# Normalised causal convolution over 16 channels: VectorE's third of the streamed units given to ScalarE and GpSimd

## The chip, the cores and the metric

The kernel runs on one core of one Trainium2 chip. The metric is the device time of one execution in microseconds; of three executions of the kernel before the median is 2928.14 us.

## What is computed

The input `x` has 16 channels of 2048 x 2048 in fp32. Channels form 8 groups of 2. The reference, cut to what matters:

```python
# layer 0
xm = where(tril, gn(x), 0)                      # gn: mean and variance over a group of 2 channels
y  = depthwise_conv(xm, weight, 6 x 11 taps)    # one filter per channel
x1 = x + where(tril, y, 0)
# layer 1
bias[h, i, j] = table(i - j)[h]                 # a small MLP of the position difference
out = x1 + gn(x1) + bias
```

The second normalisation is a scale and an offset per group, so `out = x1 * s + (bias + o)`. Above the diagonal the convolution is zero and `x1` is `x`.

## The kernel before

**Stages.** The program runs over stages, one per group and a few more. In a stage three groups are in work: the statistics of group s (`do_a`), normalisation and convolution of group s-1 (`do_b`), and the output of group s-2 (`do_c`). Stages 2 to 6 are one loop body, executed five times; stages 0, 1, 7, 8 and 9 are written out. Stages 0 and 1 produce no output, 8 has no statistics, and 9, the tail, only finishes output of the last group. A steady stage is called a lap below.

**Positions.** A stage has 90 positions n, one for each convolution tile of a group (2 channels, 4 bands of 512 rows, strips of columns). Each engine's program is written position by position, and each engine works it off in order. At position n ScalarE casts the transposed tile n+2 (L560), normalises tile n+4 (L545), squares finished pieces (L582), and then handles the output of group s-2. VectorE makes the low halves of tile n+2 (L696), masks and adds the convolution of tile n-1 (L709, L711), and then finishes output and takes statistics of `abuf` (L724). GpSimd masks tile n+4 where the diagonal runs through it (`mask_tile`, L940), copies the halo columns (L963, L955) and then adds bias (L971). TensorE transposes (L1022) and convolves (L1036) tile by tile, three tiles in flight.

**Output units.** Parts of `x1` that are kept in SBUF are finished in place by VectorE (`finish_kept`, L863, "kept blocks"), stored, and their place reloaded for the next group. All else is streamed: 36 units of 512 KB per group go through a ring of four buffers `ubuf` (`NUB`). SP loads a unit (L473) once the unit four before it in the ring has been stored. Then there are two ways to finish it:

- on ScalarE and GpSimd: `scale_stream` (L602, ScalarE, times s) and `add_bias` (L971, GpSimd, plus bias), stored from ScalarE's queue two positions later;
- on VectorE: `finish_stream` (L871), one instruction that does both, stored one position later.

The store itself is `store_stream` (L609) on ScalarE's queue, with a wait for the unit's finish. At one position ScalarE's program has the scalings first and the stores behind them. All queues are strictly in order, SP's too.

**What sets the order.** The table of constants before `plan` gives positions. `plan` spreads the loads, the uses and the stores of the units over the positions with a budget of bytes per position; a unit's position is `p.u[u]`, its load two positions before it or as soon as the store of unit u-4 is past. `U_ON_DVE(n, u)` says which way a unit takes. It is evaluated once for a steady lap and the same choice holds in every stage. These lines depend on it:

```python
p.u_load.append(max(at - 2, p.u_store[u - NUB] + 1) if u >= NUB else 0)
p.on_dve.append(on_dve[u] if on_dve else U_ON_DVE(p.u[u], u))
p.u_store.append(min(p.u[u] + (1 if p.on_dve[u] else 2), NT - 1))
```

In a group 13 units are VectorE's: 3, 7, 11, 15, 17, 19, 23, 27, 29, 31, 33, 34, 35. The last two are at position 87. The reload of the bias table (`load_bias`, L507, SP) waits for all additions and finishes of a channel.

Of the kernel before, what the change touches and what calls it, by code (L numbers as in the profile page):

```python
# [25 lines left out]
def preact_conv_kernel(nc, x, wflip, w1, b1, w2, b2, w3, b3, out):  # L26
# [84 lines left out]

    U_WEIGHT = lambda n: 1.8 if n < 10 else 1.5 if n > 82 else 1.0

    U_ON_DVE = lambda n, u: n > 85 or (u % 2 == 1 if n > 78 or 36 < n < 42 else u % 4 == 3)
    NEXT_BIAS_LOAD = 89


# [46 lines left out]
    def plan(do_a, do_b, do_c, on_dve=None):  # L164
# [40 lines left out]
        if do_c:  # L205
            for c, (lo, hi) in enumerate(U_WINDOW):
                for at in spread(NU // 2, 1.0, lo, hi, U_WEIGHT if do_a else lambda n: 1.0):
                    u = len(p.u)
                    p.u_load.append(max(at - 2, p.u_store[u - NUB] + 1) if u >= NUB else 0)
                    p.u.append(min(max(at, p.u_load[u] + 1, p.u[-1] if u else 0), hi))  # L210
                    p.on_dve.append(on_dve[u] if on_dve else U_ON_DVE(p.u[u], u))
                    p.u_store.append(min(p.u[u] + (1 if p.on_dve[u] else 2), NT - 1))
# [906 lines left out]
```

## Time and profile before

| | |
|---|---|
| median of 3 executions | 2928.14 us (2927.49 to 2932.59) |
| the profiled execution | 2927.91 us |
| its span | 2926.2 us |
| VectorE busy | 2305.1 us (79%) |
| TensorE matmul busy | 2044.5 us (70%) |
| ScalarE busy | 1674.6 us (57%) |
| GpSimd busy | 1158.7 us (40%) |
| DMA traffic | 916.61 MB, 313 GB/s in the mean |
| L602 and L971, each | 184 instructions |
| L871 | 104 instructions |

An engine's busy share says how much of the span it had an instruction in work. A row of the trace gives the start, the duration and, in brackets, how long the engine had been idle before and what released it. The rows used stand in a section below.

### The profile page before, as it was taken

What the parts mean: (1) busy time and instruction counts of PE and PEld (TensorE: products, weight loads), DVE (VectorE), ACT (ScalarE), POOL (GpSimd) and SP (SyncE); (2) the same over time, 40 slices, a digit from 0 to 9 for tenths busy, and PEclk for the clock granted to TensorE, in tenths of its full rate; (3) what the DMA queues carried; (4) which work ended last, traced back from release to release, by engine and by line L of the source; (5) the groups of instructions that cost most, each with busy time, mean ns of one, the idle gap of its engine ahead of it and who ended that gap; (6) DMA issues with size and microseconds to landing.
All of it is one profiled execution on the core that took longest, in us unless ns stands there. A gap on an engine that the chain in (4) does not pass through costs nothing.

```text
span 2926.2 us, 81475 instructions
## 1 busy us (share of the span) xinstructions
PE 2044.5 (70%) x28880; PEld 1944.5 (66%) x28880; DVE 2305.1 (79%) x4167; ACT 1674.6 (57%) x3051; POOL 1158.7 (40%) x1988
## 2 busy tenths in 40 slices
PE   4098887876677776777768876787767778888600
PEld 0098877776677776777657776776767777787500
DVE  6788888788778888789788887878987886767624
ACT  2066665656466665666456565575656666676621
POOL 1033234534335343543345344353434534454433
PEclk9999998999788898999889897899989998899855
DMA  8885749998699987989789997999889895878798
GB/s 260 293 303 164 285 149 382 364 328 329 241 367 350 367 323 293 376 326 358 277 334 363 326 345 252 367 363 358 311 315 370 332 349 197 311 255 295 280 342 331
DMA packets 316269, 916.61 MB, mean 313 GB/s; under 512 B 39280, under 2 KB 39280, under 8 KB 313936
## 3 DMA queue, kind: packets, MB, share of 16 engines
q1 hardware_dynamic: 201952, 595.03, 56.9%
q10 hardware_dynamic: 114048, 318.80, 28.7%
q8 instruction: 71, 1.16, 0.2%
q14 instruction: 198, 1.62, 0.2%
HBM read 594.18 MB, written 319.68 MB: 312 GB/s over the span
## 4 chain that ended last, share of the span: by engine, by line
DMA 38%; DVE 26%; issue 15%; PE 8%; ACT 6%; POOL 2%; SPq 2%; ACTq 1%; DVEq 0%; POOLq 0%
DMA ubuf<-in_x 11%; DMA out<-kept_c_band 9%; DVE entries L724 9%; DMA out<-ubuf 7%; PE psY L1036 6%; DVE kept_c_band L863 4%; DVE XT L696 4%; DMA ubuf<-out 4%; DMA abuf<-in_x 3%; DVE psY L709 3%; DMA kept_c_band<-in_x 3%; DVE kept_c_band L711 2%; ACT junk L582 2%; PE psT L1022 2%; ACT XT L560 2%
## 5 line engine op out<-in xcount | busy, mean ns | idle before, releaser
L1036 PEld LDWEIGHTS psY<-wsplit,XT 128*128 128x128 f16 x25920 | 1658.2, 103 | 291.7 <-DVE band L711 87.1
L1036 PE MATMUL psY<-wsplit,XT 128*128 128x168 f16 (+5 forms) x25920 | 1680.7, 226 | 233.7 <-DVE kept_c_band L711 98.8
L696 DVE TENSOR_TENSOR XT<-psT,XT 128x512 f16<-128x512 f32 x720 | 491.8, 683 | 372.4 <-ACT XT L560 370.5
L1022 PE MATMUL psT<-ident,xn 128*128 128x128 f32 x2880 | 500.9, 301 | 355.3 <-POOL xn L940 261.1
L560 ACT CAST XT<-psT 128x512 f16<-128x512 f32 x720 | 414.1, 575 | 455.6 <-PE psT L1022 260.1
L971 POOL TENSOR_TENSOR ubuf<-ubuf,bias 128x1024 f32<-128x1024 f32 x184 | 415.4, 2258 | 573.4 <-ACT ubuf L602 572.5
L724 DVE BATCH_NORM_STATS2 entries<-abuf 128x6 f32<-128x512 f32 x928 | 589.5, 682 | 62.4 <-DMA abuf<-in_x 61.3
L940 POOL TENSOR_TENSOR xn<-xn,mask 128x512 f32<-128x512 f32 x336 | 422.8, 1258 | 517.7 <-ACT xn L545 439.5
L1022 PEld LDWEIGHTS psT<-ident,xn 128*128 128x128 f32 x2880 | 331.6, 151 | 369.4 <-POOL xn L940 263.5
L545 ACT ACTIVATE xn<-kept_c_band,normp 128x512 f32<-128x512 f32 (+2 forms) x496 | 398.5, 803 | 109.3 <-DMA kept_c_band<-in_x 75.8
L963 POOL COPY halo<-XT 128x16 f16<-128x16 f16 x720 | 209.8, 291 | 634.1 <-DVE XT L696 619.3
L602 ACT ACTIVATE ubuf<-ubuf,outp 128x1024 f32<-128x1024 f32 x184 | 210.1, 1143 | 338.0 <-DMA ubuf<-in_x 228.5
L863 DVE SCALAR_TENSOR_TENSOR kept_c_band<-kept_c_band,outp,bias 128x1024 f32<-128x1024 f32 x224 | 348.6, 1569 | 38.8 <-ACT bias L652 38.8
L582 ACT ACTIVATE junk<-kept_c_band,cur 128x512 f32<-128x512 f32 (+2 forms) x464 | 311.9, 672 | 78.4 <-DVE kept_c_band L711 42.2
L711 DVE SCALAR_TENSOR_TENSOR kept_c_band<-psY,wback,kept_c_band 128x472 f32<-128x472 f32 (+3 forms) x496 | 344.6, 695 | 6.2
L871 DVE SCALAR_TENSOR_TENSOR ubuf<-ubuf,outp,bias 128x1024 f32<-128x1024 f32 x104 | 153.8, 1484 | 114.5 <-DMA ubuf<-in_x 64.2
L709 DVE TENSOR_TENSOR psY<-psY,mask 128x472 f32<-128x472 f32 (+2 forms) x336 | 204.1, 607 | 0.0
L545 ACT ACTIVATE xn<-band,normp 128x512 f32<-128x512 f32 (+1 forms) x224 | 174.3, 779 | 34.9 <-DVE normp L790 34.9
L955 POOL COPY XT<-halo 128x16 f16<-128x16 f16 x720 | 167.2, 232 | 27.3 <-PE psY L1036 23.2
L582 ACT ACTIVATE junk<-band,cur 128x512 f32<-128x512 f32 x192 | 131.9, 687 | 44.4 <-DVE cur L795 21.3
L711 DVE SCALAR_TENSOR_TENSOR band<-psY,wback,band 128x472 f32<-128x472 f32 (+2 forms) x224 | 150.5, 672 | 5.7
L582 ACT ACTIVATION_READ_ACCUMULATOR junk<-kept_c_band,cur 128x1 f32 x464 | 87.1, 188 | 0.0
(76 smaller groups left out, 445.0 us busy)
## 6 DMA issues: line engine op xcount, KB each, us to landing
abuf<-in_x SPq DMA_DIRECT2D x464, 512.0 KB, 7.3
out<-ubuf ACTq DMA_DIRECT2D x288, 512.0 KB, 6.4
kept_c_band<-in_x SPq DMA_DIRECT2D x112, 1024.0 KB, 7.8
out<-kept_c_band ACTq DMA_DIRECT2D x112, 1024.0 KB, 7.8
ubuf<-in_x SPq DMA_DIRECT2D x192, 512.0 KB, 6.3
band<-in_x SPq DMA_DIRECT2D x48, 1024.0 KB, 9.7
out<-band ACTq DMA_DIRECT2D x48, 1024.0 KB, 7.9
ubuf<-out SPq DMA_DIRECT2D x96, 512.0 KB, 6.6
```

Source lines behind the costliest of these rows:

```text
L545: last = nc.scalar.activation(to[:, :, 0:whole, :], slot(c, b)[:, :, x0:x0 + XC * whole].rearrange("p k (i c) -> p k i c", c=XC), ACT.Iden ...
L560: nc.scalar.copy(XT[:, n % NB3, 0, :, 2:P + 2], psT[n % NB3][:, :, :]).then_inc(hi_ready, 1)
L582: nc.scalar.activation(junk[:, 0:nr * (c1 - c0)].rearrange("p (r c) -> p r c", r=nr), slot(c, b)[:, r:r + nr, BW * q + c0:BW * q + c1], AC ...
L696: nc.vector.tensor_tensor(XT[:, n % NB3, 1, :, 2:P + 2], psT[n % NB3][:, :, :], XT[:, n % NB3, 0, :, 2:P + 2], ALU.subtract).then_inc(lo_r ...
L709: nc.vector.tensor_tensor(y, y, mask_at(b, t, c0, c1), ALU.mult).then_inc(conv_masked, 1)
L711: nc.vector.scalar_tensor_tensor(out=xs, in0=y, scalar=col(wback, c), in1=xs, op0=ALU.mult, op1=ALU.add, accum_out=sums[:, n:n + 1]).then_ ...
L724: last = nc.vector.bn_stats(entries[:, e, :], row(q, r))
L863: nc.vector.scalar_tensor_tensor(out=v, in0=v, scalar=col(outp, 0), in1=bias_at(blk, nr // 2 * h, nr // 2), op0=ALU.mult, op1=ALU.add).the ...
L940: nc.gpsimd.tensor_tensor(v, v, m, ALU.mult).then_inc(xn_ready, 1)
L971: nc.gpsimd.tensor_tensor(v, v, bias_at(STREAM[u]), ALU.add).then_inc(u_added, 1)
L1022: last = nc.tensor.transpose(psT[m][:, i, :], xn[:, m, i, :, :].rearrange("p k c -> p (k c)"), ident[:, :])
L1036: last = nc.tensor.matmul(psY[m][:, 0:rows, o + lo_c:o + hi_c], XT[:, m, xp, i, 2 - sh:2 - sh + P], wsplit[:, c, wp, K * sh:K * sh + rows, ...
```

## The change

One line. Units at positions up to 85, 34 of 36 in a group, are scaled by ScalarE and get their bias from GpSimd; the last two stay on VectorE.

```diff
-    U_ON_DVE = lambda n, u: n > 85 or (u % 2 == 1 if n > 78 or 36 < n < 42 else u % 4 == 3)
+    U_ON_DVE = lambda n, u: n > 85
```

Eleven units of each group change their way: 3, 7, 11, 15, 17, 19, 23, 27, 29, 31, 33. Their stores move one position back, and through `plan` the loads of units 31, 33 and 35 move one position back and a few loads of `abuf` by one or two positions. The instructions themselves are those that other units already use.

ScalarE's program in the loop body, at positions 80 and 81 (L560 cast and L545 norm open a position, L602 scales a unit, L609 stores one; the ISA and REGISTER_ALU rows are waits and register updates). Before:

```order
L560 CAST XT<-psT 128x4x128
L545 ACTIVATE xn<-kept_c_band,normp 128x4x4x32
L601 ISA
L602 ACTIVATE ubuf<-ubuf,outp 128x1024
L608 REGISTER_ALU
L609 ISA
L609 DMA out<-ubuf 128x1024
L554 REGISTER_ALU
L560 CAST XT<-psT 128x4x128
L545 ACTIVATE xn<-kept_c_band,normp 128x4x4x32
```

Now:

```order
L560 CAST XT<-psT 128x4x128
L545 ACTIVATE xn<-kept_c_band,normp 128x4x4x32
L601 ISA
L602 ACTIVATE ubuf<-ubuf,outp 128x1024
L554 REGISTER_ALU
L560 CAST XT<-psT 128x4x128
L545 ACTIVATE xn<-kept_c_band,normp 128x4x4x32
L602 ACTIVATE ubuf<-ubuf,outp 128x1024
L608 REGISTER_ALU
L609 ISA
L609 DMA out<-ubuf 128x1024
```

The store of unit 27 stood behind the scaling of unit 28 and now stands a tile later, behind the scaling of unit 29, which is new here.

VectorE's program at position 74 of the loop body, around unit 23 (L871 finishes it, L764 aggregates the statistics). Before:

```order
L711 SCALAR_TENSOR_TENSOR kept_c_band,sums<-psY,wback,kept_c_band 128x4x118
L869 ISA
L871 SCALAR_TENSOR_TENSOR ubuf<-ubuf,outp,bias 128x1024
L760 ISA
L761 REGISTER_ALU
L762 MEMSET t 128x1
L764 BN_AGGR t<-entries 128x2
```

Now:

```order
L711 SCALAR_TENSOR_TENSOR kept_c_band,sums<-psY,wback,kept_c_band 128x4x118
L760 ISA
L761 REGISTER_ALU
L762 MEMSET t 128x1
L764 BN_AGGR t<-entries 128x2
```

The finish and its wait for the load (L869) are gone from VectorE, and nothing stands in their place.

The end of ScalarE's program in the tail (the last two pairs of stores are those of units 32 and 33, and of 34 and 35). Before:

```order
L602 ACTIVATE ubuf<-ubuf,outp 128x1024
L609 DMA out<-ubuf 128x1024 x2
L602 ACTIVATE ubuf<-ubuf,outp 128x1024
L609 DMA out<-ubuf 128x1024 x3
L602 ACTIVATE ubuf<-ubuf,outp 128x1024
L609 DMA out<-ubuf 128x1024 x2
L609 DMA out<-ubuf 128x2x512 x2
```

Now:

```order
L602 ACTIVATE ubuf<-ubuf,outp 128x1024
L609 DMA out<-ubuf 128x1024
L602 ACTIVATE ubuf<-ubuf,outp 128x1024
L609 DMA out<-ubuf 128x1024
L602 ACTIVATE ubuf<-ubuf,outp 128x1024
L609 DMA out<-ubuf 128x1024
L602 ACTIVATE ubuf<-ubuf,outp 128x1024
L609 DMA out<-ubuf 128x1024 x2
L609 DMA out<-ubuf 128x2x512 x2
```

Two or three stores stood together behind one scaling; now nearly each store has a scaling ahead of it, with that unit's wait for its load.

## Rows read from the trace of the kernel before

**Rows 1.** The page: busy time by engine, and the chain by engine.

```profile
PE 2044.5 (70%) x28880; PEld 1944.5 (66%) x28880; DVE 2305.1 (79%) x4167; ACT 1674.6 (57%) x3051; POOL 1158.7 (40%) x1988
...
DMA 38%; DVE 26%; issue 15%; PE 8%; ACT 6%; POOL 2%; SPq 2%; ACTq 1%; DVEq 0%; POOLq 0%
```

**Rows 2.** Groups of instructions: busy us, mean ns | idle us before, releasers.

```profile
L696 DVE TENSOR_TENSOR XT<-psT,XT 128x512 f16<-128x512 f32 x720 | 491.8, 683 | 372.4 <-ACT XT L560 370.5
...
L560 ACT CAST XT<-psT 128x512 f16<-128x512 f32 x720 | 414.1, 575 | 455.6 <-PE psT L1022 260.1
L971 POOL TENSOR_TENSOR ubuf<-ubuf,bias 128x1024 f32<-128x1024 f32 x184 | 415.4, 2258 | 573.4 <-ACT ubuf L602 572.5
...
L602 ACT ACTIVATE ubuf<-ubuf,outp 128x1024 f32<-128x1024 f32 x184 | 210.1, 1143 | 338.0 <-DMA ubuf<-in_x 228.5
...
L863 DVE SCALAR_TENSOR_TENSOR kept_c_band<-kept_c_band,outp,bias 128x1024 f32<-128x1024 f32 x224 | 348.6, 1569 | 38.8 <-ACT bias L652 38.8
...
L871 DVE SCALAR_TENSOR_TENSOR ubuf<-ubuf,outp,bias 128x1024 f32<-128x1024 f32 x104 | 153.8, 1484 | 114.5 <-DMA ubuf<-in_x 64.2
```

**Rows 3.** Windows: us, busy PE, PEld, DVE, ACT, POOL; PEclk, DMA share, GB/s.

```profile
1097.90:1444.20 346.30, 255.10 (x3606) 245.24 (x3606) 285.71 (x521) 207.16 (x380) 143.93 (x247) 0.89 0.89 331
...
1209.00:1259.00 50.00, 40.36 (x603) 38.52 (x601) 37.44 (x70) 38.83 (x72) 30.02 (x43) 0.94 0.99 389
...
1374.00:1395.00 21.00, 18.08 (x294) 17.80 (x292) 20.93 (x38) 16.98 (x31) 9.51 (x17) 1.00 0.91 333
1395.00:1433.00 38.00, 23.41 (x302) 22.75 (x300) 27.34 (x50) 19.54 (x37) 18.48 (x27) 0.82 0.79 292
...
2750.20:2926.20 176.00, 5.35 (x91) 5.16 (x88) 74.45 (x74) 37.79 (x42) 56.03 (x24) 0.52 0.89 324
```

**Rows 4.** Timeline of one lap: ScalarE at position 10, VectorE at 41.

```profile
1152.30 0.81 ACT L545 ACTIVATE xn<-kept_c_band,normp 128x512 f32<-128x512 f32 x1 [7.79 <-DMA kept_c_band<-in_x]
...
1256.11 2.16 DVE L871 SCALAR_TENSOR_TENSOR ubuf<-ubuf,outp,bias 128x1024 f32<-128x1024 f32 x1
```

**Rows 5.** DMA issues of the ring: KB each, median us to landing.

```profile
out<-ubuf ACTq DMA_DIRECT2D x288, 512.0 KB, 6.4
...
ubuf<-in_x SPq DMA_DIRECT2D x192, 512.0 KB, 6.3
```

**Rows 6.** Lines L863 and L871: minimum, median and maximum duration in ns.

```profile
L863 DVE SCALAR_TENSOR_TENSOR kept_c_band<-kept_c_band,outp,bias x224: 1272/1282/3377, 432.2 to 2878.8; 128x1024 f32<-128x1024 f32 x112
...
L871 DVE SCALAR_TENSOR_TENSOR ubuf<-ubuf,outp,bias x104: 1272/1285/3279, 453.5 to 2921.4; 128x1024 f32<-128x1024 f32 x104
```

**Rows 7.** Timeline of VectorE, positions 81 to 87 of that lap.

```profile
1400.59 1.42 DVE L871 SCALAR_TENSOR_TENSOR ubuf<-ubuf,outp,bias 128x1024 f32<-128x1024 f32 x1
...
1409.78 2.24 DVE L871 SCALAR_TENSOR_TENSOR ubuf<-ubuf,outp,bias 128x1024 f32<-128x1024 f32 x1 [3.25 <-DMA ubuf<-in_x]
...
1416.52 0.70 DVE L711 SCALAR_TENSOR_TENSOR kept_c_band<-psY,wback,kept_c_band 128x472 f32<-128x472 f32 x1
...
1429.99 1.32 DVE L871 SCALAR_TENSOR_TENSOR ubuf<-ubuf,outp,bias 128x1024 f32<-128x1024 f32 x1
```

**Rows 8.** Timeline of ScalarE's queue at position 80: the store of unit 27.

```profile
1397.91 0.34 ACTq L609 DMA_DIRECT2D out<-ubuf  x1
```

**Rows 9.** Timeline of SP's queue: the load of unit 31.

```profile
1405.34 0.33 SPq L473 DMA_DIRECT2D ubuf<-in_x  x1
```

**Rows 10.** Transfers of the ring from 1385 to 1445: stores, then loads.

```profile
DMA to landing us min/median/max: 2.9/4.2/11.5
...
ubuf<-in_x SPq DMA_DIRECT2D x8, 512.0 KB, 5.5
```

**Rows 11.** Timeline of the tail's end: units 31, 35 (VectorE) and 32 (ScalarE).

```profile
2908.41 1.29 DVE L871 SCALAR_TENSOR_TENSOR ubuf<-ubuf,outp,bias 128x1024 f32<-128x1024 f32 x1 [6.83 <-DMA ubuf<-in_x]
...
2921.36 1.28 DVE L871 SCALAR_TENSOR_TENSOR ubuf<-ubuf,outp,bias 128x1024 f32<-128x1024 f32 x1 [3.40 <-DMA ubuf<-in_x]
...
2910.47 1.15 ACT L602 ACTIVATE ubuf<-ubuf,outp 128x1024 f32<-128x1024 f32 x1 [6.19 <-DMA ubuf<-in_x]
```

## The prediction

> **What bounds the kernel now.** I read the page first [rows 1], then the groups of instructions [rows 2], the windows of single laps and stretches [rows 3], and last the instructions and transfers of the stretches that decide [rows 4 to 11]. A measurement of this kernel can tell about 0.2% (5.9 us) from no change. The profiled execution took 2927.91 us, 1.7 us more than its span, and lies 0.2 us under the median, so I count against it.
>
> No engine is full: VectorE is busy 79% of the span, and the chain that ended last is 38% DMA and 26% VectorE [rows 1]. A steady lap takes 346.3 us [rows 3], with VectorE at 285.7, ScalarE at 207.2, GpSimd at 143.9 and the DMA engines at 0.89. The kernel changes its bound several times in a lap. VectorE is the bound where it has no gap: 20.93 of 21.0 us from 1374 to 1395 [rows 3]. From 1209 to 1259 the DMA share is 0.99 and VectorE has 12.6 us free; from 1395 to 1433 it has 10.7 free. There the ring of four streamed buffers sets the pace: unit u+4 is loaded only when unit u is stored. It shows as waits for `ubuf` loads in front of L602 (338.0 us idle, of which at least 228.5 <-DMA in_x) and in front of L871 (114.5 idle) [rows 2].
>
> **What the change moves.** Of 13 units per group that VectorE finishes, 11 go to the other pair, 88 in the run. Their positions in a steady lap are 9, 27, 33, 38, 41, 49, 74, 79, 81, 83, 85. With the means of [rows 2]: VectorE loses 88 x 1.484 = 130.6 us, ScalarE gains 88 x 1.143 = 100.6, GpSimd 88 x 2.258 = 198.7. Busy time alone makes no engine full: per lap 16.3 us off VectorE, ScalarE to 220, GpSimd to 169. Nothing is added to the DMA traffic. But two things get later for each moved unit. Its finish takes 1.14 + 2.26 = 3.4 us instead of 1.48, and its store stands one position later in ScalarE's queue. And the wait for its load is now on ScalarE: what stands behind it there, the store of an earlier unit, the cast of the next tile and the norm four tiles ahead, waits too. The sum, stretch by stretch:
>
> 1. **Position 9, 0 us.** ScalarE next waits 7.79 us for a kept block's load [rows 4]; VectorE's 1.28 us are hidden by that DMA. If that load came early they would show: bound -1.3.
>
> 2. **Positions 27 to 41, +1 us a lap.** VectorE's gaps come from ScalarE waiting for ring loads, so freed time is worth nothing until 41. The store of unit 10 moves behind the scaling of unit 11, the store of 11 behind that of 13, the stores of 14 and 15 behind those of 15 and 16: 3 to 6 us later each, if I add the 6.4 and 6.3 us medians of a store and a load [rows 5]. At a DMA share of 0.99 these transfers queue, and one issued later waits less. At 41 VectorE had a 2.16 us instruction [rows 4] just where it becomes the bound, and that goes; its successor on ScalarE (1.14) and GpSimd (2.26, ahead of the mask and halo copy of the next tile) fills about the same time. I take +1, bounds -1 and +4.
>
> 3. **Position 49, -0.6 us.** VectorE is the bound; 1.28 us go. The load came long before. But the addition now runs on GpSimd beside L863 of positions 49 and 50. The rows show what that does: L863 and L871 have medians of 1.282 and 1.285 and means of 1.569 and 1.484, with 2.16 at position 41 [rows 2, 4, 6]. Half of the gain is what I leave. By the Trainium skill ("SBUF — State Buffer", Who interferes with whom) a VectorE instruction with two SBUF inputs and a GpSimd instruction that reads SBUF exclude each other for a whole instruction, whoever starts first; the trace agrees in kind (1.28 against 2.16). By that rule, an addition that always starts first costs 2.26 - 1.28 = +1.0 us here in place of -0.6, and the sum would be 2952.
>
> 4. **Position 74, 0 us.** 1.28 us of VectorE work (the median of [rows 6]) go, ahead of the long aggregation. The scaling now on ScalarE makes the store of unit 22 later, and the load of 26 waits for that one. Behind it the ring is the bound again, so the gain ends there. Bound -1.3.
>
> 5. **Positions 79 to 85, +1 us.** Today the store of unit 27 is issued at 1397.91, behind the scaling of unit 28 [rows 8]. Now it stands behind the scaling of 29, which can't start before that load is there; VectorE started unit 29 at 1400.59 [rows 7]: +2.7. Load 31 waits for this store; it was issued at 1405.34 [rows 9] and used, after a wait for it, at 1409.78 [rows 7], 4.4 us. It now comes at about 1412.5. Then the two paths part. On VectorE, today 2.24 us of L871, a unit of statistics and the chain of the norm's root stand between the load and L711 at 1416.52 [rows 7], 6.7 us. After the change only scaling, cast and split stand there, 1.14 + 0.58 + 0.68 = 2.4 us [rows 2], since VectorE does its other work while it waits: L711 at 1414.9, 1.6 us earlier, and TensorE is released by it. But ScalarE waits from there on: the store of 29 goes out at 1412.5 and no longer two positions earlier; with 4.2 us for a store and 5.5 for a load in this stretch [rows 10], load 33 lands at 1422.2, and only behind its scaling are 30 and 31 stored, whose buffers units 34 and 35 need. They come at about 1432, where VectorE used them at 1429.99 [rows 7]: +2.2. Of -1.6 and +2.2 the later path ends the lap, less what its successors can hide: I take +1. With the run's medians (6.4 and 6.3) the second path is +8; bounds -1.6 and +5.
>
> A lap: 0 + 1 - 0.6 + 0 + 1 = +1.4 us. There are seven laps with tiles and streamed units; x 7 = +9.8, say +10.
>
> 6. **The tail, +3 us.** The last 176 us [rows 3] only finish units; each is taken the moment its load lands. Most moved units cost nothing there, since their store already stands behind the next unit's scaling. Not so at the end [rows 11]. Unit 31's load lands at 2908.41, 32's at 2910.47. Today 31 is finished by VectorE at 2909.7 and stored; now by GpSimd at 2908.4 + 1.1 + 2.3 = 2911.8, +2.1, and load 35 waits for that store. So the last unit, at 2921.36 today, is at 2923.4. Bias reload in mid-tail waits for unit 17's addition, +1. Bounds +1 and +8.
>
> Sum: 2927.9 + 10 + 3 = **2941 us**.
>
> **The rivals.**
> - **A, VectorE's relief is what counts.** For it: 79% busy, and no gap at 41, 49 and 74. 2.16 + 1.28 + 1.28 = 4.7 us a lap, x 7 = 33, tail +3: 2898. Against it: a ring-bound stretch follows each of these. It decides if the ring's loads come earlier as the laps get shorter.
> - **B, it is all absorbed.** DMA share 0.89 in a lap [rows 3]: what one stretch loses the queue makes up in the next, and only the tail shows: 2931, within 0.2%.
> - **C, the ring costs in full.** If later stores are not made up by shorter queues, stretches 2 and 5 pay +4 and +5: (9 - 0.6) x 7 + 3 = 62, so 2990. It decides once fewer transfers in flight leave the DMA engines idle; the 0.79 share from 1395 to 1433 [rows 3] speaks for it, the 0.99 from 1209 on against.
> - **D, GpSimd in VectorE's way at 49.** By rows: 2.26 on GpSimd ahead of L863 against 1.28 saved, +1.0 where I have -0.6, seven laps and as much again for positions 41 and 74: +11 to +12, 2953. This is the rule named under 3. Against it: GpSimd's moved instructions take the place of VectorE's own two-input ones, whose blocked share was 88 x (1.484 - 1.285) = 17.5 us.
> - That the change does nothing can be excluded: the listing shows the moved instructions.
>
> **How the numbers follow.** Forecast (slower by a little, 2934 to 2960): 0.33. A: 0.26. B: 0.24. C: 0.12. D: 0.05. So faster 0.26, same 0.24, slower 0.50. Cases of both signs hold most of the chance; the likeliest one's own range is 2934 to 2960. The range over all starts at 2900, which leaves out the lower half of A around its 2898, and ends at 2975, a little beyond the middle of C and D.
>
> **What would show it.** Right: L871 x16, L971 and L602 x272 at nearly their means; L602's idle time for DMA up by roughly the 114.5 us that stood before L871; steady laps of 345 to 350 us; from store of 27 to load of 31 about 3 us later; L863's mean near 1.57; a tail of 178 to 182. Wrong: steady laps under 340 us (A), over 352 (C), or L863's mean over 1.7 (D). If the windows corresponding to 1395 to 1433 are shorter than 38 us, step 5 has the wrong sign.

## The result and the profile after

The changed kernel takes 2968.31 us (median of 4 executions, 2958.84 to 2977.99) against 2927.81 us (4 executions, 2923.30 to 2932.59) for the kernel before: ratio 1.0138, 95% interval 1.0102 to 1.0175. It is slower by 40.5 us. The forecast was 2941 with a range over all of 2900 to 2975; the range of the forecast's own case was 2934 to 2960.

The page and the groups of instructions of the changed kernel: busy time by engine, the chain by engine, then busy us, mean ns | idle us before, releasers.

```profile
PE 2038.4 (69%) x28880; PEld 1933.5 (65%) x28880; DVE 2179.5 (73%) x4079; ACT 1762.8 (59%) x3139; POOL 1302.3 (44%) x2076
...
DMA 37%; DVE 22%; issue 17%; ACT 9%; PE 7%; POOL 4%; SPq 2%; ACTq 2%; DVEq 0%; POOLq 0%
...
L971 POOL TENSOR_TENSOR ubuf<-ubuf,bias 128x1024 f32<-128x1024 f32 x272 | 603.0, 2218 | 616.1 <-ACT ubuf L602 614.8
L724 DVE BATCH_NORM_STATS2 entries<-abuf 128x6 f32<-128x512 f32 x928 | 588.0, 681 | 80.8 <-DMA abuf<-in_x 79.3 <-issue 0.6
L696 DVE TENSOR_TENSOR XT<-psT,XT 128x512 f16<-128x512 f32 x720 | 491.2, 682 | 530.1 <-ACT XT L560 529.8
L863 DVE SCALAR_TENSOR_TENSOR kept_c_band<-kept_c_band,outp,bias 128x1024 f32<-128x1024 f32 x224 | 358.7, 1615 | 86.2 <-ACT bias L652 86.2
L602 ACT ACTIVATE ubuf<-ubuf,outp 128x1024 f32<-128x1024 f32 x272 | 310.2, 1141 | 362.3 <-DMA ubuf<-in_x 244.7 <-DMA ubuf<-out 87.9 <-DVE kept_c_band L863 13.7
L871 DVE SCALAR_TENSOR_TENSOR ubuf<-ubuf,outp,bias 128x1024 f32<-128x1024 f32 x16 | 22.5, 1406 | 57.8 <-DMA ubuf<-in_x 57.8
```

Against [rows 1, 2], VectorE lost 125.6 us of work (2305.1 to 2179.5), and more than that came back as waiting. It now waits 157.7 us longer for ScalarE's casts ahead of L696 (530.1, was 372.4), 47.4 us longer for the scaled bias (86.2, was 38.8), and 18.4 us longer for statistics loads ahead of L724; ahead of L871 it waits 56.7 us less. The four give +166.8 us, which is the 125.6 us of work that went and the 41.2 us by which the span grew (2926.2 to 2967.4). L724's group in the kernel before:

```profile
L724 DVE BATCH_NORM_STATS2 entries<-abuf 128x6 f32<-128x512 f32 x928 | 589.5, 682 | 62.4 <-DMA abuf<-in_x 61.3 <-issue 0.6
```

Windows of the changed kernel: three steady laps, the last with tiles, and the tail (columns as in [rows 3]).

```profile
763.80:1112.60 348.80, 255.17 (x3606) 245.32 (x3606) 267.77 (x510) 217.98 (x392) 161.93 (x258) 0.89 0.90 329
1112.60:1463.20 350.60, 253.28 (x3606) 242.63 (x3606) 269.52 (x509) 217.87 (x391) 162.46 (x258) 0.91 0.90 326
1463.20:1817.60 354.40, 257.09 (x3606) 246.12 (x3606) 267.24 (x510) 217.84 (x392) 162.97 (x258) 0.89 0.89 324
...
2497.20:2792.20 295.00, 234.90 (x3456) 226.58 (x3454) 186.91 (x350) 208.52 (x372) 160.94 (x249) 0.92 0.75 268
2792.20:2967.40 175.20, 5.11 (x88) 4.92 (x85) 64.95 (x63) 50.23 (x52) 79.22 (x35) 0.52 0.88 325
```

The lap of [rows 3] grew from 346.3 to 350.6 us; over all seven laps with tiles the growth is 39.4 us. The tail is 0.8 us shorter (175.2, was 176.0).

**Where in the lap.** I cut every lap of a timeline at the starts of L696 of tile n+2 and summed each stretch over the seven laps. The table shows, for the one profiled execution of each kernel, the difference to the kernel before in us. The labels are those of the experiments below.

| positions | after | e1 | e2 | e3 | e4 | e5 | e6 | e7 | e8 | f1 | f2 | f3 | f4 |
|---|---|---|---|---|---|---|---|---|---|---|---|---|---|
| 0 to 27 | -6.9 | -1.9 | 0.6 | 7.7 | -2.6 | 0.8 | 1.5 | -1.5 | -5.1 | 4.3 | -3.1 | 0.4 | -2.4 |
| 27 to 42 | 8.7 | 10.1 | -3.2 | -3.1 | -1.2 | 7.2 | 1.3 | -10.9 | -0.5 | 3.0 | 11.6 | -3.5 | -3.9 |
| 42 to 48 | 6.3 | 6.7 | -1.4 | 6.3 | 7.1 | -0.6 | 7.1 | -0.5 | 6.6 | 0.0 | -1.4 | -1.4 | 1.4 |
| 48 to 54 | -7.1 | -8.5 | -7.3 | -12.0 | -1.9 | -13.3 | 1.1 | -8.6 | -15.5 | -15.0 | -13.3 | -0.2 | -16.9 |
| 54 to 72 | 13.6 | 14.4 | 0.6 | 40.1 | 10.7 | 6.4 | 4.4 | 4.2 | 13.5 | 5.9 | 4.4 | 3.5 | 8.9 |
| 72 to 78 | -3.3 | -8.0 | -0.8 | -6.5 | -0.9 | -10.4 | -0.2 | -10.2 | -7.3 | -10.5 | -7.9 | 1.1 | -8.7 |
| 78 to 90 | 28.1 | 0.3 | 18.5 | -3.0 | 2.9 | 15.8 | 3.6 | -9.1 | 25.2 | 3.4 | 6.2 | -1.6 | 5.7 |

A difference of 3.5 us in such a sum also appears where nothing was edited (27 to 42 in f3, whose one edit lies behind it), so a single profiled execution can't tell less. The profiled executions are not the medians either: that of the kernel before, 2927.91 us, is 3 to 5 us above the medians of its later groups, those of e2, e4, e5 and f3 are the fastest of their kernels and those of e3 and e7 the slowest. The table says where time goes; how much a change costs is read from the ratios of the experiments.

**Three places that decide.** First the ring at the end of the lap. Timeline of the changed kernel, ScalarE and its queue with the additions and finishes that its stores wait for, from the addition of unit 27 to the cast after the last store (rows of L871 are units 34 and 35, the double row of L971 units 30 and 31):

```profile
1411.27 2.36 POOL L971 TENSOR_TENSOR ubuf<-ubuf,bias 128x1024 f32<-128x1024 f32 x1 [3.42 <-ACT ubuf L602]
...
1419.61 1.15 ACT L602 ACTIVATE ubuf<-ubuf,outp 128x1024 f32<-128x1024 f32 x1 [2.40 <-DMA ubuf<-out]
1419.82 0.34 ACTq L609 DMA_DIRECT2D out<-ubuf  x1
...
1427.47 4.68 POOL L971 TENSOR_TENSOR ubuf<-ubuf,bias 128x1024 f32<-128x1024 f32 x2 [1.19 <-ACT ubuf L602]
...
1440.28 1.15 ACT L602 ACTIVATE ubuf<-ubuf,outp 128x1024 f32<-128x1024 f32 x1 [4.66 <-DMA ubuf<-in_x]
1440.48 0.91 ACTq L609 DMA_DIRECT2D out<-ubuf  x2
...
1447.97 1.28 DVE L871 SCALAR_TENSOR_TENSOR ubuf<-ubuf,outp,bias 128x1024 f32<-128x1024 f32 x1 [0.66 <-DMA ubuf<-in_x]
...
1451.44 1.28 DVE L871 SCALAR_TENSOR_TENSOR ubuf<-ubuf,outp,bias 128x1024 f32<-128x1024 f32 x1 [2.19 <-DMA ubuf<-in_x]
...
1453.47 0.58 ACT L560 CAST XT<-psT 128x512 f16<-128x512 f32 x1 [5.07 <-DVE ubuf L871]
```

Unit 27's addition was over at 1413.6; its store left at 1419.82, when the scaling of unit 29 was released. Units 30 and 31 were finished by 1432.2 and left at 1440.5, behind the scaling of 33, which had waited 4.66 us for its load. So units 34 and 35 landed when VectorE already stood waiting, and their stores, waiting on ScalarE's queue for L871, held a cast for 5.07 us. This is the path of step 5; in the kernel before VectorE took unit 34 without any wait [rows 7]. It is not the whole of the 28.1 us at 78 to 90. The change also moves loads of `abuf`, 14 of the 58 in a lap: ten of them one or two positions back, and four (numbers 5 to 8), at positions 81 to 87 of the lap before their use, one to three positions forward, among these ring loads (the section on the change said one or two positions for all). With the later stores and `abuf` as before (e5) the stretch is 15.8 us longer, with the moved loads of `abuf` alone (e6) 3.6 us; only both together give the 28.1. How the four loads add to the delay of the ring is not shown.

Second, the gap at position 46, where ScalarE scales the bias table (L652, 3.27 us) and VectorE must wait for the cast behind it. Before:

```profile
1273.08 1.28 DVE L724 BATCH_NORM_STATS2 entries<-abuf 128x6 f32<-128x512 f32 x2
...
1276.65 0.69 DVE L696 TENSOR_TENSOR XT<-psT,XT 128x512 f16<-128x512 f32 x1 [2.29 <-ACT XT L560]
```

After:

```profile
1293.48 0.69 DVE L696 TENSOR_TENSOR XT<-psT,XT 128x512 f16<-128x512 f32 x1 [3.49 <-ACT XT L560]
...
1296.61 2.46 DVE L724 BATCH_NORM_STATS2 entries<-abuf 128x6 f32<-128x512 f32 x4
```

Two operations of statistics used to run inside the wait. The planner has moved them one position on, behind it, and the wait is 1.20 us longer. In the table it is 42 to 48: every kernel in which this load of `abuf` (number 41) is used a position later (after, e1, e3, e4, e6 and e8) pays 6.3 to 7.1 us there, 0.9 to 1.0 us a lap, and no other does.

Third, position 66. In the changed kernel a load of `abuf` (number 52) and its use are one position later, the load among the ring's:

```profile
1366.72 1.29 DVE L724 BATCH_NORM_STATS2 entries<-abuf 128x6 f32<-128x512 f32 x2 [1.70 <-DMA abuf<-in_x]
1368.06 1.15 ACT L602 ACTIVATE ubuf<-ubuf,outp 128x1024 f32<-128x1024 f32 x1 [5.98 <-DMA ubuf<-in_x]
```

VectorE now waits 1.70 us for statistics, and ScalarE 5.98 us for its unit, 4.45 us in the kernel before:

```profile
1349.50 1.15 ACT L602 ACTIVATE ubuf<-ubuf,outp 128x1024 f32<-128x1024 f32 x1 [4.45 <-DMA ubuf<-in_x]
```

### The profile page after: what moved, and what is told of

It reads as the page before. It is cut to its first block, busy times and chain, and to the rows that moved or that the text cites. A ratio compares the mean times of both kernels' runs of the same rounds, so it can differ in the third digit from the quotient of the medians.

```text
span 2967.4 us, 81510 instructions
## 1 busy us (share of the span) xinstructions
PE 2038.4 (69%) x28880; PEld 1933.5 (65%) x28880; DVE 2179.5 (73%) x4079; ACT 1762.8 (59%) x3139; POOL 1302.3 (44%) x2076
## 3 DMA queue, kind: packets, MB, share of 16 engines
q8 instruction: 71, 1.16, 0.2%
## 4 chain that ended last, share of the span: by engine, by line
DMA 37%; DVE 22%; issue 17%; ACT 9%; PE 7%; POOL 4%; SPq 2%; ACTq 2%; DVEq 0%; POOLq 0%
DMA ubuf<-in_x 11%; DMA out<-kept_c_band 8%; DVE entries L724 8%; DMA out<-ubuf 7%; PE psY L1036 5%; DVE kept_c_band L863 4%; DVE XT L696 3%; DMA abuf<-in_x 3%; DMA ubuf<-out 3%; DMA kept_c_band<-in_x 3%; DVE psY L709 3%; ACT junk L582 3%; ACT XT L560 2%; ACT xn L545 2%; DVE kept_c_band L711 2%
## 5 line engine op out<-in xcount | busy, mean ns | idle before, releaser
L696 DVE TENSOR_TENSOR XT<-psT,XT 128x512 f16<-128x512 f32 x720 | 491.2, 682 | 530.1 <-ACT XT L560 529.8
L971 POOL TENSOR_TENSOR ubuf<-ubuf,bias 128x1024 f32<-128x1024 f32 x272 | 603.0, 2218 | 616.1 <-ACT ubuf L602 614.8
L560 ACT CAST XT<-psT 128x512 f16<-128x512 f32 x720 | 413.1, 574 | 398.1 <-PE psT L1022 219.8
L724 DVE BATCH_NORM_STATS2 entries<-abuf 128x6 f32<-128x512 f32 x928 | 588.0, 681 | 80.8 <-DMA abuf<-in_x 79.3
L940 POOL TENSOR_TENSOR xn<-xn,mask 128x512 f32<-128x512 f32 x336 | 422.4, 1257 | 426.1 <-ACT xn L545 365.7
L602 ACT ACTIVATE ubuf<-ubuf,outp 128x1024 f32<-128x1024 f32 x272 | 310.2, 1141 | 362.3 <-DMA ubuf<-in_x 244.7
L545 ACT ACTIVATE xn<-kept_c_band,normp 128x512 f32<-128x512 f32 (+2 forms) x496 | 398.5, 803 | 126.9 <-DMA kept_c_band<-in_x 86.2
L963 POOL COPY halo<-XT 128x16 f16<-128x16 f16 x720 | 182.9, 254 | 586.6 <-DVE XT L696 574.4
L863 DVE SCALAR_TENSOR_TENSOR kept_c_band<-kept_c_band,outp,bias 128x1024 f32<-128x1024 f32 x224 | 358.7, 1615 | 86.2 <-ACT bias L652 86.2
L545 ACT ACTIVATE xn<-band,normp 128x512 f32<-128x512 f32 (+1 forms) x224 | 174.3, 779 | 6.1 <-DVE normp L790 6.1
L955 POOL COPY XT<-halo 128x16 f16<-128x16 f16 x720 | 156.8, 218 | 25.7 <-PE psY L1036 22.9
L652 ACT ACTIVATE bias<-bias,outp 128x3587 f32<-128x3587 f32 x16 | 52.4, 3277 | 41.7 <-DVE outp L839 31.3
```

The lines of the kernel that those rows point to most:

```text
L545: last = nc.scalar.activation(to[:, :, 0:whole, :], slot(c, b)[:, :, x0:x0 + XC * whole].rearrange("p k (i c) -> p k i c", c=XC), ACT.Iden ...
L560: nc.scalar.copy(XT[:, n % NB3, 0, :, 2:P + 2], psT[n % NB3][:, :, :]).then_inc(hi_ready, 1)
L602: nc.scalar.activation(v, v, ACT.Identity, scale=col(outp, 0)).then_inc(u_scaled, 1)
L696: nc.vector.tensor_tensor(XT[:, n % NB3, 1, :, 2:P + 2], psT[n % NB3][:, :, :], XT[:, n % NB3, 0, :, 2:P + 2], ALU.subtract).then_inc(lo_r ...
L724: last = nc.vector.bn_stats(entries[:, e, :], row(q, r))
L863: nc.vector.scalar_tensor_tensor(out=v, in0=v, scalar=col(outp, 0), in1=bias_at(blk, nr // 2 * h, nr // 2), op0=ALU.mult, op1=ALU.add).the ...
```

## The experiments

Twelve kernels ran in three groups; the kernel before was timed with each: 2925.11 us (10 executions) beside e1 to e4, 2922.81 (11) beside e5 to e8, 2924.16 (35) beside f1 to f4. Ratios are to it, with 95% intervals. Where a kernel pins the loads of `abuf`, its line numbers are 2 lower than in the changed kernel.

**e1, late units back.**

```diff
-    U_ON_DVE = lambda n, u: n > 85
+    U_ON_DVE = lambda n, u: n > 85 or (n > 78 and u % 2 == 1)
```

> The four units of a group behind position 78 (27, 29, 31, 33) are VectorE's again, the seven earlier ones stay with ScalarE and GpSimd. Theory L (the cost is made at positions 79 to 87, where scalings that wait for ring loads stand ahead of the stores that these loads wait for): about 2938 us, 10 over the kernel before, and positions 84 to 90 as long as before. Rival S (every moved unit costs about the same 0.46 us, by the longer finish and the fuller ScalarE and GpSimd): 7/11 of 40 us, 2954.

Measured: 2942.19 us, ratio 1.0080 (1.0048 to 1.0112). That is nearer to Theory L's 2938 than to the rival's 2954.

**e2, late units only**, from the kernel before.

```diff
-    U_ON_DVE = lambda n, u: n > 85 or (u % 2 == 1 if n > 78 or 36 < n < 42 else u % 4 == 3)
+    U_ON_DVE = lambda n, u: n > 85 or (n <= 78 and (u % 2 == 1 if 36 < n < 42 else u % 4 == 3))
```

> Only units 27, 29, 31 and 33 are moved. Theory L: about 2958 us, three quarters of the 40 us, with positions 84 to 90 some 5 us longer in every lap. Rival S: 4/11 of 40 us, 2943.

Measured: 2937.43 us, 1.0059 (1.0034 to 1.0084), below both expectations (2958 and 2943). The two halves add up within their intervals (0.80 + 0.59%, against 1.38%), so the loss doesn't sit in the late units alone; an interplay of a few tenths of a per cent is not excluded, and in the table the two give 18.8 us at 78 to 90 against 28.1. There e1 has lost the 28 us at 78 to 90 and keeps those before; e2 is roughly the mirror image.

**e3, store ahead of scaling** in ScalarE's program of a position, from the changed kernel.

```diff
+                            if p.u_store[u] == n:
+                                store_stream(gc, u)
+                        for u in range(NU):
...
-                        for u in range(NU):
-                            if p.u_store[u] == n:
-                                store_stream(gc, u)
```

> The changed kernel with one swap in ScalarE's program: at each position the stores that are due come first and the scalings behind them. Theory L in its narrow form (a store that is ready is held by a scaling that waits for its load): most of the cost goes, 2940 us or less. Rival W (what costs is that ScalarE itself waits, and so casts and norms come late, whatever the order of the stores): stays at 2960 to 2970.

Measured: 2957.79 us, 1.0108 (1.0076 to 1.0140), between the two expectations and near the rival's. The held stores at the end are cured (78 to 90: -3.0 for +28.1), but 54 to 72 costs 40.1 for 13.6. Two rows of ScalarE in that stretch, 3.21 and 5.98 us in the changed kernel:

```profile
1335.08 0.81 ACT L545 ACTIVATE xn<-kept_c_band,normp 128x512 f32<-128x512 f32 x1 [8.34 <-DMA kept_c_band<-in_x]
...
1367.96 1.15 ACT L602 ACTIVATE ubuf<-ubuf,outp 128x1024 f32<-128x1024 f32 x1 [8.94 <-DMA ubuf<-in_x]
```

There the loads land later than their use by more; why they do is open. So the 28 us at the end of the lap go when the stores come first, and this order gives most of the gain back elsewhere; the two totals, 1.0138 and 1.0108, are not apart by their intervals.

**e4, all stores late**, from the kernel before.

```diff
-                    p.u_store.append(min(p.u[u] + (1 if p.on_dve[u] else 2), NT - 1))
+                    p.u_store.append(min(p.u[u] + 2, NT - 1))
```

> The kernel before, with the stores of VectorE's units also two positions after their use instead of one. No instruction changes its engine. Theory L: the ring gets slower by the later stores alone, 2938 to 2950 us. Rival W: within 0.2% of the kernel before, 2922 to 2934.

Measured: 2945.03 us, 1.0080 (1.0051 to 1.0110), inside Theory L's range, which doesn't yet show its mechanism. The stretch 78 to 90 grew by 2.9 us only, but 42 to 48 by 7.1 and 54 to 72 by 10.7. This pointed to something that I had not priced: the plan books the stores' bytes before it places the loads of `abuf`, and moves 22 of these 58 loads here, 14 in the changed kernel, 10 in e1 and 4 in e2. So e4 mixes two causes, and the next pair takes one of them by itself.

**e5, loads of `abuf` as before**, from the changed kernel; **e6** is the reverse, the kernel before with the changed kernel's lists. The diff for e5 (lists cut):

```diff
-            for at in spread(NA, 0.5, A_LO, A_END - 2, lambda n: 1.0):
-                a = len(p.a)
-                p.a_load.append(max(at, p.a[a - NAB] + 1) if a >= NAB else at)
-                p.a.append(min(p.a_load[a] + 2, A_END))
+            p.a_load = [-16, -15, ..., 36, 39, 40, 41, 41, 42, 44, ..., 63, 65, 66, 66, 67, 68]
+            p.a = [-14, -13, ..., 38, 41, 42, 43, 43, 44, 46, ..., 65, 67, 68, 68, 69, 70]
```

> The changed kernel, with the loads and uses of abuf at the positions that they had before the change (written out as a table). Theory P (the planner books the later stores, and so moves loads of abuf, one of them from position 63 to 64, ahead of the ring load of unit 21; that makes positions 54 to 72 longer): 2950 to 2957 us, ratio 1.009 to 1.011. Rival (those shifts are harmless, all of the cost is in the finish of the moved units): as the changed kernel, ratio 1.014.

> The kernel before, with the loads and uses of abuf where the changed kernel has them, and nothing else. Theory P: 10 to 15 us slower than before, ratio 1.0035 to 1.005. Rival: no difference.

Measured: e5 2932.39 us, 1.0042 (1.0025 to 1.0060); e6 2943.89 us, 1.0063 (1.0028 to 1.0097). The shifted loads are worth 1.0138 - 1.0042 = 0.96%, 28 us, in the changed kernel, more than Theory P had expected, and 0.63%, 18 us, in the kernel before. 0.42% is left for engines and stores. Loads and uses moved together in every run, so which of the two costs is not shown, but for position 46, where it is the use.

**e7, VectorE's relief by itself**: the kernel before, where VectorE's finish of the eleven units is a copy of one element, with all waits. The scaling and bias of these units are left out.

```diff
+                if u < 34:
+                    nc.vector.tensor_copy(v[:, 0, 0:1], v[:, 0, 0:1]).then_inc(u_finished, 1)
+                else:
...
```

> The kernel before, but on VectorE the 11 units are not finished: one element per partition is copied in place after the same waits (these units are left without scale and bias), so only the 130 us of work go. If the laps are bound by the ring and by DMA around these units (my forecast): 0 to 12 us faster. Rival A (VectorE's relief counts where it has no gap): 30 us or more faster.

Measured: 2880.20 us, 0.9839 (0.9814 to 0.9865). The relief is worth 1.61%, 47 us: Rival A was right on this, and my forecast of 0 to 12 us was not. It comes at 27 to 42 (-10.9), at 48 to 54 (-8.6), at 72 to 78 (-10.2) and at 78 to 90 (-9.1).

**e8, the moved work by itself**: the changed kernel, where scaling and addition of the eleven units handle one element per partition or one element per row, so that their scaling and bias are left out too.

```diff
-                v = ubuf[:, u % NUB, :, :]
+                v = ubuf[:, u % NUB, :, 0:1] if u in MOVED else ubuf[:, u % NUB, :, :]
...
+                if u in MOVED:
+                    nc.gpsimd.tensor_tensor(v[:, 0, 0:1], v[:, 0, 0:1], v[:, 0, 0:1], ALU.add).then_inc(u_added, 1)
+                else:
...
```

> The changed kernel, with the scaling and the addition of the 11 moved units cut to one element per partition, all waits and their order kept (these units are left without scale and bias). Theory W (what costs is the order of waits and stores, not the work): still 25 us or more over the kernel before. Rival (the 1.14 us on ScalarE and 2.2 us on GpSimd are the cost): within 10 us of the kernel before, or faster.

Measured: 2951.34 us, 1.0091 (1.0059 to 1.0123). The durations of the moved instructions are 0.47% (+-0.5), 14 us, of the loss, which is barely told from nothing. Without them the changed order alone is 0.91% slower than the kernel before, as Theory W expected, with VectorE relieved all the same: 78 to 90 still costs 25.2 us. What costs in the changed kernel is mainly where the stores and loads stand.

**f1, late units back and `abuf` as before; f2, units 11, 15 and 17 back as well; f3, the kernel before with one load of `abuf` later; f4, the changed kernel with the stores where the kernel before has them.** The edits, f1 and f2 on top of e5, f3 as in e5 on the kernel before with 64 for 63 and 66 for 65:

```diff
-    U_ON_DVE = lambda n, u: n > 85
+    U_ON_DVE = lambda n, u: n > 85 or (n > 78 and u % 2 == 1)              # f1
+    U_ON_DVE = lambda n, u: n > 85 or u in (11, 15, 17, 27, 29, 31, 33)    # f2
```

```diff
+    WAS_ON_DVE = lambda n, u: n > 85 or (u % 2 == 1 if n > 78 or 36 < n < 42 else u % 4 == 3)
...
-                    p.u_store.append(min(p.u[u] + (1 if p.on_dve[u] else 2), NT - 1))
+                    p.u_store.append(min(p.u[u] + (1 if WAS_ON_DVE(p.u[u], u) else 2), NT - 1))
```

> The changed kernel with the loads and uses of abuf where the kernel before has them, and units 27, 29, 31 and 33 back on VectorE; units 3, 7, 11, 15, 17, 19 and 23 stay moved. Theory S (three separate terms: the shifted abuf loads, some 28 us; the held stores of the late units, some +33 us at tiles 84 to 90 against a relief of -17 us at 81 to 84; the rest): the abuf term is gone as in e5 (2932) and the late units' net +16 to +26 as well, so 2906 to 2918 us, below the kernel before (2925). Theory N (the two parts are not additive, the laps are refilled by another wait): 2925 to 2935.

> As f1, and units 11, 15 and 17 (positions 33, 38, 41) back on VectorE too, so that only 3, 7, 19 and 23 are moved, where the stretches of e5 showed no loss (48 to 54: -13 us in seven laps; 33 to 39: +18 us, 39 to 42: -6 us). Theory S: 5 to 12 us below f1, 2898 to 2912. Theory N, or a relief of VectorE at 33 to 41 that outweighs what the ring loses there: equal to f1 or above it, up to 2930.

> The kernel before with one load of abuf (number 52) a position later, 64 in place of 63, and its use at 66 in place of 65. Theory O (that load now stands beside unit 21's ring load and its two BN_STATS operations land on the busy stretch 66 to 72, where e6 lost 12 us and the changed kernel 15 us): 2933 to 2940 us, the loss between tiles 66 and 72. Rival (the loss of e6 is spread over its some fifteen shifted loads): 2922 to 2928.

> The changed kernel with the stores of the eleven moved units one position after their finish, as in the kernel before, which also gives back before's ring loads and abuf loads; only the engines differ. Theory R (what costs is the ring place held a tile longer by the later store): the +33 us of e5 at tiles 84 to 90 shrinks to under +10, and the time is 2905 to 2918. Theory Q (what costs is the chain scaling, addition, store itself, 0.98 + 2.2 us in place of one operation of 1.6 us, and now ScalarE's queue waits for the addition): no gain on e5, 2930 to 2950, with ScalarE's waits ahead of the stores growing.

| | median us (12 executions) | ratio | interval |
|---|---|---|---|
| f1 | 2919.33 | 0.9978 | 0.9957 to 0.9998 |
| f2 | 2922.26 | 0.9981 | 0.9960 to 1.0002 |
| f3 | 2936.25 | 1.0032 | 1.0010 to 1.0055 |
| f4 | 2910.95 | 0.9949 | 0.9929 to 0.9969 |

f1 came out a microsecond above Theory S's range and below the kernel before; Theory S missed for f2, which came out as Theory N had it: moving fewer units gave nothing more. f3 agrees with Theory O in its median. The place shows in its profile as in the changed kernel's:

```profile
1352.80 1.29 DVE L722 BATCH_NORM_STATS2 entries<-abuf 128x6 f32<-128x512 f32 x2 [1.84 <-DMA abuf<-in_x]
1354.13 1.15 ACT L600 ACTIVATE ubuf<-ubuf,outp 128x1024 f32<-128x1024 f32 x1 [6.11 <-DMA ubuf<-in_x]
```

Its size does not: the profiled execution took 2921.18 us, the fastest of the twelve, and 54 to 72 is 3.5 us longer in it. What the other eleven spent more is open, and so is whether the loss lies where Theory O has it.

f4 is the fastest of the kernels that do the whole work, 0.5% faster than the kernel before and 1.9% faster than the changed one, with the changed kernel's engines for the same units. In the laps all its stores, ring loads and loads of `abuf` stand where the kernel before has them; in the last two stages three stores (unit 34's in each, and unit 29's in the tail) stand a position later. Its chain and groups (lines here are 1 higher):

```profile
DMA 27%; DVE 26%; issue 20%; PE 10%; ACT 7%; POOL 7%; SPq 2%; ACTq 1%; POOLq 0%; DVEq 0%
...
L603 ACT ACTIVATE ubuf<-ubuf,outp 128x1024 f32<-128x1024 f32 x272 | 309.9, 1141 | 298.6 <-DMA ubuf<-in_x 176.9 <-DMA ubuf<-out 78.9 <-POOL ubuf L972 23.6
```

and its timeline where units 27 and 31 are added and stored:

```profile
1385.93 2.36 POOL L972 TENSOR_TENSOR ubuf<-ubuf,bias 128x1024 f32<-128x1024 f32 x1 [6.09 <-ACT ubuf L603]
...
1388.45 0.34 ACTq L610 DMA_DIRECT2D out<-ubuf  x1
1388.97 0.58 ACT L561 CAST XT<-psT 128x512 f16<-128x512 f32 x1 [0.90 <-POOL ubuf L972]
...
1400.64 4.67 POOL L972 TENSOR_TENSOR ubuf<-ubuf,bias 128x1024 f32<-128x1024 f32 x2 [1.19 <-ACT ubuf L603]
...
1405.47 0.34 ACTq L610 DMA_DIRECT2D out<-ubuf  x1
```

The store of 27 leaves 0.2 us after its addition ends, at the price of 0.90 us in which ScalarE's cast waits. The scalings wait 298.6 us for their units in place of 362.3 in the changed kernel and 330.7 in e5, and DMA's share of the chain is 27%, against 37 and 38%. Theory R's time holds (2905 to 2918), and Theory Q, which saw no gain on e5, falls, though the wait for the addition that it names exists. (Its sizes were off: by the rows it is 1.14 and 2.20 us in place of 1.48.) Theory R's place holds in part: at tiles 84 to 90, where e5 is 33.0 us longer than the kernel before, f4 still is by 18.5, not by under 10. The difference of e5 and f4, the same loads of `abuf` with the stores one position later (and the ring loads of 31, 33 and 35 that follow from them), is 1.0042 - 0.9949 = 0.93%, 27 us. In the table it lies about equally at 27 to 42 (11.1 us) and at 78 to 90 (10.1 us).

## Why the prediction was right in direction and short in size

The account by ratios, in per cent of 2926 us: other engines for eleven units, all else in its place, -0.51 (f4), -15 us; their stores one position later, +0.93 (e5 over f4), +27 us; the loads of `abuf` that the plan moves because of it, +0.96 (changed kernel over e5), +28 us. Sum +1.38%, +40 us. The intervals of these terms are about +-0.2, +-0.27 and +-0.4 of a per cent. They add up because each kernel starts from the one before it; taken in another order the terms can be of other sizes, as the 0.63% of e6 for the loads of `abuf` shows. The change lost because of what a rule beside the changed line attaches to the engine, a later store, and not because of the engines: with the stores left in place the same engines for the same units are faster than the kernel before.

- **Slower, 2934 to 2960, with chance 0.33:** the sign was right and the range over all, 2900 to 2975, held the 2968.3; the forecast's own case, 2934 to 2960, did not. The sum 2927.9 + 10 + 3 has no term for the loads of `abuf`, although the diff's effect on them stood in the section on the change. This is the step that failed: it was put at nothing, without a reason, and measured 28 us. That the range over all still held is partly luck, since its upper end was there for Rivals C and D. Luck also is in the sum itself: e5, the changed kernel without the shifted loads, is at +0.42%, 12 us, beside the 13 us of the sum, but steps 3, 4 and 6 gained more than I had put down and step 5 lost more.
- **Step 1, position 9, 0 us:** -6.9 for 0 to 27, -1.0 a lap, inside the bound of -1.3. That it is the relief of position 9 is not shown: e1 and e5, which move unit 3 too, have -1.9 and +0.8.
- **Step 2, positions 27 to 41, +1 a lap:** 27 to 42 grew by 8.7 / 7 = 1.2 a lap. Right in the changed kernel. Where the stores are early (f4) the sign turns, -0.6.
- **Step 3, position 49, -0.6 a lap:** -7.1 / 7 = -1.0; with `abuf` in place -13.3 / 7 = -1.9 (e5). Too small; see the next section for the part that is not relief.
- **Step 4, position 74, 0, bound -1.3:** the finish's time did show; the stretch of tiles 72 to 75 was 1.1 us shorter a lap, and 72 to 78 shrank by 8.0 to 10.5 us in e1, e5 and f1. In the changed kernel the ring gave back all but 3.3.
- **Step 5, positions 79 to 85, +1, bounds -1.6 and +5:** the mechanism was right, event by event (store of 27 behind the scaling of 29, stores of 30 and 31 behind that of 33, late units 34 and 35). The size was not: 78 to 90 is 28.1 / 7 = +4.0 a lap, of which 15.8 / 7 = 2.3 stays with `abuf` in place (e5). The waits of the scalings of units 29, 32 and 33 for their loads (2.40, 2.60 and 4.66 us in the lap shown) follow on one another in the ring instead of being hidden, and the cast that waits 5.07 us behind the last store was not in my path.
- **Step 6, the tail, +3, bounds +1 and +8:** -0.8. The wrong sign: below its lower bound.
- **Rival A, the relief counts:** priced at 4.7 x 7 = 33 us. e7 gives 47, so the relief was underrated. It did not decide: with all else in place the work on ScalarE and GpSimd takes 1.10%, 32 us, of it back (0.9949 of f4 - 0.9839 of e7), and the two placement terms are larger than the rest. **Rival B** falls. **Rival C:** the five steady laps took 345.2 to 354.7 us, two of them in the forecast's 345 to 350 and two over Rival C's 352; it priced stretch 5 nearly (+5 against +4.0, for a part of which the loads of `abuf` are the reason) and stretch 2 too high (+4 against +1.2). **Rival D:** L863's mean went from 1.569 to 1.615, far under 1.7, though the block does occur (below).
- **The signs I named:** counts and means of L602, L971 and L871 came as said. L602's wait for DMA did not rise by 114.5: its idle time rose by 24.3 (338.0 to 362.3), and 57.8 stayed in front of the 16 L871. VectorE's wait for loads became its wait for ScalarE ahead of L696. The tail of 178 to 182 us did not come (175.2). From the start of position 78 on (1388.51 before, 1405.88 after), the store of 27 comes 4.5 us later (1397.91 and 1419.82) and the load of 31 2.1 us (1405.34 and 1424.83), where I had said about 3. The end of the lap got longer, so step 5 had the right sign.

## What to carry to other kernels

When a change gives work to another engine, look for rules that hang on the engine: a store position, a booked byte. Here the exchange itself gained 0.5%, and a rule next to it cost 1.9%. Hold the rest of the plan fixed first, then let it move. Compare every list that the planner writes, not only those that the diff names. Two statistics operations that left a wait at position 46 cost 0.9 to 1.0 us a lap of their 1.28, and a ring with four places paid 27 us for eleven stores a group that stood one tile later.

## What the runs showed of the hardware that I had not expected

A VectorE operation with two inputs in SBUF and a GpSimd operation that reads SBUF held each other up, by the order in which they happen to start. Kernel before at position 50, VectorE and GpSimd:

```profile
1293.18 1.99 DVE L863 SCALAR_TENSOR_TENSOR kept_c_band<-kept_c_band,outp,bias 128x1024 f32<-128x1024 f32 x1
...
1292.95 1.13 POOL L940 TENSOR_TENSOR xn<-xn,mask 128x512 f32<-128x512 f32 x1 [3.25 <-ACT xn L545]
```

e2, the same two instructions, which its edit doesn't touch:

```profile
1293.69 1.28 DVE L863 SCALAR_TENSOR_TENSOR kept_c_band<-kept_c_band,outp,bias 128x1024 f32<-128x1024 f32 x1
...
1293.78 2.18 POOL L940 TENSOR_TENSOR xn<-xn,mask 128x512 f32<-128x512 f32 x1 [3.56 <-ACT xn L545]
```

Whoever starts second takes 0.7 to 1.05 us longer (1.99 for 1.28, 2.18 for 1.13). On VectorE, which bounds this stretch (15.20 us busy of 15.31), that shows (15.31 us for tiles 48 to 51 before, 14.60 in e2); on GpSimd it is hidden. A shift of 0.3 us between the engines is thus worth 0.7 us a lap at each such place, and e2's -7.3 at 48 to 54 is this alone: in its five steady laps L863 takes 1.28 us in place of some 1.99 at two positions. The Trainium skill ("SBUF — State Buffer", Who interferes with whom) says that the two exclude each other for a whole instruction, whoever starts first, and these rows agree to within 0.2 us: 0.90 us of L940 was left when L863 started and L863 took 0.71 longer; 1.19 of L863 was left when L940 started and L940 took 1.05 longer. I had used the rule for the added instructions only. A longer block stood in the changed kernel, an addition begun 0.64 us ahead of L863, which then took 1.16 us more:

```profile
1300.90 2.44 DVE L863 SCALAR_TENSOR_TENSOR kept_c_band<-kept_c_band,outp,bias 128x1024 f32<-128x1024 f32 x1
...
1300.26 1.99 POOL L971 TENSOR_TENSOR ubuf<-ubuf,bias 128x1024 f32<-128x1024 f32 x1
```

In f4 the same addition ran beside four operations of statistics, which read one operand each, and neither was longer: 1.99 and 2.46 us, where four such operations also take 2.46 or 2.47 us in the changed kernel.

```profile
1275.58 2.46 DVE L725 BATCH_NORM_STATS2 entries<-abuf 128x6 f32<-128x512 f32 x4
...
1275.68 1.99 POOL L972 TENSOR_TENSOR ubuf<-ubuf,bias 128x1024 f32<-128x1024 f32 x1
```
